# Two rounded passes for the log-decay product, in a fused gated-delta and FP4 feed-forward layer

## The reference, cut to what matters

```python
beta = sigmoid(x @ b_w.T + b_bias + beta_bias) * 2.0
g = -exp(A_log) * softplus(x @ a_w.T + dt_bias)
def step(S, inp):
    q_t, k_t, v_t, g_t, b_t = inp
    S = S * exp(g_t)[..., None, None]
    mem = einsum('bhk,bhkv->bhv', k_t, S)
    delta = (v_t - mem) * b_t[..., None]
    S = S + einsum('bhk,bhv->bhkv', k_t, delta)
    o_t = einsum('bhk,bhkv->bhv', q_t, S)
    return (S, o_t)
```

## Time and profile before

| | us |
|---|---|
| median of 3 runs | 3399.68 (3399.31 to 3400.36) |
| profiled execution, its own time | 3392.96 |
| its span, first to last instruction | 3391.1 |
| PE busy | 3166.5 (93% of the span) |
| VectorE (DVE) busy | 2422.4 (71%) |
| GpSimd (POOL) busy | 1847.1 (54%) |
| ScalarE (ACT) busy | 1671.9 (49%) |

### The profile page before, as it was taken

The page is one execution under the profiler, slowest core; times in us unless marked ns, Lnnn a source line. Parts: engine busy times, 40 slices in busy tenths (PEclk is TensorE's granted clock), DMA queues, the critical chain, the costliest instruction groups (busy, mean ns, idle before and its releaser), DMA issues.

```text
span 3391.1 us, 118358 instructions
## 1 busy us (share of the span) xinstructions
PE 3166.5 (93%) x45632; PEld 2248.8 (66%) x45632; DVE 2422.4 (71%) x5407; ACT 1671.9 (49%) x3306; POOL 1847.1 (54%) x2737
## 2 busy tenths in 40 slices
PE   5899999999999999999999999999999999999995
PEld 4666666766666766666666666666667666666664
DVE  7677776777777777767777767777777777777772
ACT  3544554545554445545445545455545455544452
POOL 3465445665455664456654456654556654466543
PEclk8999999999999999999999999999999999999996
DMA  3111111111111111111111111111111111111111
GB/s 109 39 45 27 35 42 34 45 39 27 39 37 40 45 33 30 42 33 45 45 27 36 42 33 45 40 29 36 42 36 45 35 27 42 36 42 45 27 30 29
DMA packets 318317, 132.07 MB, mean 39 GB/s; under 512 B 277089, under 2 KB 278881, under 8 KB 317793
## 3 DMA queue, kind: packets, MB, share of 16 engines
q1 hardware_dynamic: 313824, 119.26, 14.0%
q10 hardware_dynamic: 4096, 6.42, 0.5%
HBM read 75.30 MB, written 50.33 MB: 37 GB/s over the span
## 4 chain that ended last, share of the span: by engine, by line
POOL 32%; PE 32%; DMA 13%; issue 9%; DVE 6%; SPq 6%; POOLq 2%; ACT 1%; ACTq 0%; DVEq 0%
POOL arena L497 16%; POOL work L493 15%; PE PS L1210 7%; PE PS L1100 7%; DMA scr_a<-arena 5%; DMA arena<-scr_a 3%; PE PS L1196 3%; SPq L411 3%; SPq L393 3%; PE PS L1275 3%; DMA scr_t<-arena 2%; DMA arena<-scr_t 2%; PE PS L1228 2%; DVE arena L372 2%; PE PS L1246 2%
## 5 line engine op out<-in xcount | busy, mean ns | idle before, releaser
L874 DVE SCALAR_TENSOR_TENSOR arena<-PS,sc,arena 128x256 f32<-128x256 f32 x2112 | 1005.0, 482 | 301.9 <-ACT arena L594 201.1
L1132 PE MATMUL PS<-xh,wgu 128*128 128x256 f32 x2816 | 871.6, 341 | 36.1 <-DVE arena L874 35.6
L594 ACT ACTIVATE arena<-PS,sc 128x256 f32<-128x256 f32 x704 | 330.8, 475 | 760.0 <-PE PS L1133 703.0
L1133 PE MATMUL PS<-xl,wgu 128*128 128x256 f32 x2816 | 698.7, 281 | 0.0
L1145 PE MATMUL PS<-wdn,inner 128*128 128x512 f32 x1408 | 650.7, 592 | 0.0
L1132 PEld LDWEIGHTS PS<-xh,wgu 128*128 128x128 f32 x2816 | 531.4, 189 | 156.0 <-issue 87.4
L493 POOL TENSOR_TENSOR work<-arena 128x31 f32<-128x31 f32 (+15 forms) x992 | 517.5, 522 | 137.5 <-DMA arena<-scr_a 62.3
L1133 PEld LDWEIGHTS PS<-xl,wgu 128*128 128x128 f32 x2816 | 530.3, 188 | 83.2 <-issue 83.2
L497 POOL TENSOR_TENSOR arena<-arena,work 128x31 f32<-128x31 f32 (+15 forms) x992 | 543.1, 548 | 77.7
L1100 PE MATMUL PS<-xnT,wqkv 128*128 128x256 f32 x2048 | 494.9, 390 | 15.6 <-ACT inner L574 14.9
L1100 PEld LDWEIGHTS PS<-xnT,wqkv 128*128 128x128 f32 x2048 | 382.1, 193 | 83.8 <-ACT inner L574 15.9
(11 more groups left out here) (141 smaller groups left out, 4551.6 us busy)
## 6 DMA issues: line engine op xcount, KB each, us to landing
xt<-in_x SPq DMA_DIRECT2D x64, 256.0 KB, 2.8
scr_a<-arena SPq DMA_DIRECT2D x64, 256.0 KB, 2.4
arena<-scr_a SPq DMA_DIRECT2D x256, 64.0 KB, 3.3
obuf<-in_x SPq DMA_DIRECT2D x64, 256.0 KB, 2.8
scr_t<-arena SPq DMA_DIRECT2D x32, 512.0 KB, 2.7
arena<-scr_t SPq DMA_DIRECT2D x256, 64.0 KB, 2.3
out<-obuf SPq DMA_DIRECT2D x64, 256.0 KB, 2.0
wqkv<-in_wqkv ACTq DMA_DIRECT2D x1, 2048.0 KB, 12.9
```

The lines of the kernel that those rows point to most:

```text
L594: eng.activation(fa[:, u % 4, :], PS[:, bank(u, 0), 0:NB * P], ACT.Copy, scale=sc[:, u % 2, KB * m:KB * m + 1]).then_inc(fa_scaled.sem, 1)
L874: eng.scalar_tensor_tensor(out=fa[:, u % 4, :], in0=PS[:, bank(u, k // 2), k % 2 * NB * P:][:, 0:NB * P], scalar=sc[:, u % 2, KB * m + k:K ...
L1132: eng.matmul(o, w, xh[:, k, :], start=True, stop=False)
L1133: ins = eng.matmul(o, w, xl[:, k, :], start=False, stop=True)
```

## The change: what it does, and the diff

g is split into gh, g rounded to float32r, and gl = g - gh, which is exact and is float32r as well. Both are multiplied with the triangular mask (gm and gml), and `log_decay` becomes two float32r passes with a float32r copy of `later`, in place of one float32 product. gml lives in the buffer of xl. So xl can be made only when `log_decay` of both b has read gml, and its instruction moves from `split_x` to a new function `rest_of_x`, behind `keys_for_R` on POOL. E gets a place of its own in the arena, and gm's write then waits for `decay_out` of the tile before in place of `p_done`.

```diff
@@ -155,11 +156,12 @@
-        gm = sb("gm", [P, NB, H, CH])
-        E = gm
+        gm = sb("gm", [P, NB, H, CH], F32R)
...
+        gml = xl[:, :, :].rearrange("p k t -> p (k t)").rearrange("p (b h i) -> p b h i", b=NB, h=H)
+        E = arena[:, 9216:10240].rearrange("p (b h i) -> p b h i", b=NB, h=H)
@@ -433,15 +438,26 @@
             eng.tensor_copy(xh[:, :, :], xnT[:, :, :]).then_inc(xh_done.sem, 1)
+
+        def rest_of_x(eng, n):
+
             hold(eng, *xh_done.at(n, 1))
+            hold(eng, *decay_out.at(n, NB))
             eng.tensor_tensor(xl[:, :, :], xnT[:, :, :], xh[:, :, :].bitcast(F32), ALU.subtract).then_inc(xl_done.sem, 1)
 
         def masked_g(eng, t, n):
-            if t:
-                hold(eng, *p_done.at(t, NB))
-            for b in range(NB):
-                eng.tensor_tensor(gm[:, b, :, :], g[:, b, :].unsqueeze(2).broadcast_to([P, H, CH]),
-                                  tri[:, :].unsqueeze(1).broadcast_to([P, H, CH]), ALU.mult).then_inc(gm_done.sem, 1)
+
+            hold(eng, *g_done.at(n, 1))
+            eng.tensor_copy(gh[:, :, :], g[:, :, :]).then_inc(g_split.sem, 1)
+            hold(eng, *g_split.at(n, 1))
+            eng.tensor_tensor(gl[:, :, :], g[:, :, :], gh[:, :, :].bitcast(F32), ALU.subtract).then_inc(g_split.sem, 1)
+            hold(eng, *g_split.at(n, 2))
+            for part, dst in ((gh, gm), (gl, gml)):
+                if part is gh and t:
+                    hold(eng, *decay_out.at(t, NB))
+                for b in range(NB):
+                    eng.tensor_tensor(dst[:, b, :, :], part[:, b, :].bitcast(F32).unsqueeze(2).broadcast_to([P, H, CH]),
+                                      tri[:, :].unsqueeze(1).broadcast_to([P, H, CH]), ALU.mult).then_inc(gm_done.sem, 1)
@@ -530,6 +546,7 @@
                 expanded_g(eng, t, n)
                 masked_g(eng, t, n)
                 keys_for_R(eng, t, n)
+                rest_of_x(eng, n)
                 if more:
                     layer_norm_scale(eng, n.next())
@@ -1062,8 +1079,9 @@
             eng.tensor_copy(identb[:, :], ident[:, :]).then_inc(consts_done.sem, 1)
+            eng.tensor_copy(laterR[:, :], later[:, :]).then_inc(consts_done.sem, 1)
@@ -1160,10 +1178,11 @@
-                eng.wait_ge(*gm_done.at(n, b + 1))
+                eng.wait_ge(*gm_done.at(n, NB + b + 1))
                 eng.wait_ge(*cin_done.at(n, NQKV - 1 + b))
-                eng.matmul(PS[:, 4 + b, :], later[:, :], gm[:, b, :, :].rearrange("p h i -> p (h i)"), start=True,
-                           stop=False)
+                for part in (gm, gml):
+                    eng.matmul(PS[:, 4 + b, :], laterR[:, :], part[:, b, :, :].rearrange("p h i -> p (h i)"),
+                               start=(part is gm), stop=False)
                 eng.matmul(PS[:, 4 + b, :], identb[:, :], negm[:, :].unsqueeze(1).broadcast_to([P, H, CH]),
                            start=False, stop=True).then_inc(decay_out.sem, 1)
```

More of the change, by code:

```diff
@@ L117, in build @@
         negm = sb("negm", [P, CH], BF16)
+        laterR = sb("laterR", [P, P], F32R)
         identb = sb("identb", [P, P], BF16)
@@ L178, in build @@
         g = sb("g", [P, NB, H])
+        gh = sb("gh", [P, NB, H], F32R)
+        gl = sb("gl", [P, NB, H], F32R)
         bet = sb("bet", [P, NB, H])
@@ L205, in build @@
         t_read = signal("t_read", 128)
-        gm_done = signal("gm_done", 2)
+        g_split = signal("g_split", 2)
+        gm_done = signal("gm_done", 4)
         gx_done = signal("gx_done", 2)
@@ L1064, in _ @@
             eng.tensor_copy(identb[:, :], ident[:, :]).then_inc(consts_done.sem, 1)
+            eng.tensor_copy(laterR[:, :], later[:, :]).then_inc(consts_done.sem, 1)
             eng.tensor_tensor(biasS[:, :], bias[:, 0, :], bias[:, 1, :], ALU.add).then_inc(consts_done.sem, 1)
-            eng.wait_ge(consts_done.sem, 2)
+            eng.wait_ge(consts_done.sem, 3)
             eng.tensor_scalar(negm[:, :], tri[:, :], 1.0, 30000.0, ALU.subtract, ALU.mult).then_inc(consts_done.sem, 1)
@@ L1117, in half_unit @@
                             eng.wait_ge(wdn_done.sem, FM)
-                            eng.wait_ge(consts_done.sem, 6)
+                            eng.wait_ge(consts_done.sem, 7)
                 elif u == 1:
@@ L1467, in _ @@
             eng.wait_ge(zeroed.sem, 4)
-            eng.wait_ge(consts_done.sem, 4)
+            eng.wait_ge(consts_done.sem, 5)
             transpose_x(eng, Tile(0, 0, first=True), None)
```

## The result

The changed kernel takes 3417.45 us (median of 5 runs, 3416.7 to 3425.19) against 3399.68 for the kernel before, measured beside it: a ratio of 1.0055, 95% interval 1.0041 to 1.0070. The profiled execution took 3416.86 us, against 3392.96. It is slower by 18 us in the medians and 24 in the profiles.

The account below looks back on a forecast made before the run. The prediction took a chain through PE, DVE's state(0) and products(0), and the solve's ring as the bound. PE's saving and the masks counted nothing; xl's hold cost 0.66 us a step, 20.5 us, giving 3420, range 3398 to 3438.

Parts of the forecast that it names:

- the wait at `turn_kqn(0)`: PE's wait for DVE's product at turn_kqn(0), claimed to grow from 0.3 to 1.3 us a step.
- What bounds the kernel: Chain through PE, about five microseconds of DVE, back to PE at turn_kqn(0); delays from there to the Gram product lengthen steps.
- The passes on PE: Two float32r passes in log_decay on PE save 0.5 us a call, 1.0 us a step, 32 us of PE time.
- The cost of nothing: PE's log_decay saving was counted as nothing in the sum, since DVE's chain covers it.
- The split and the masks: Splitting g and two more masks on POOL: 3.2 us later, less 1 us from the front; nothing for the chain.
- xl's collision with `state(1)`: xl on POOL holds DVE's first update of S until 0.1 us behind xl's end: 1.65 us late.
- What comes late next: Second half of y_times_s(2) on PE waits for state(1): mean loss 0.66 us a step, times 31 steps, 20.5 us.
- The term for the stall: PE's "issue" stall in y_times_s(2), 0.76 us a step, hides under the new wait as far as it goes.
- The first: Rival: the update of S in state(1) isn't held by xl; 3400, within 3395 to 3405; chance 0.17.
- The second: Rival: PE's log_decay saving passes through, 32 us less or a part of it, 3368; chance 0.10.
- The third: Rival: low masks on POOL hold conv(2), 1.0 us a step at turn_qk(0), 32 us, 3432; chance 0.05.

Follow-up runs that it names:

- e1: The split alone against the kernel before: low part of g in its own buffer, xl made at the front as before; ratio 1.0010.
- e4: The kernel before with keys_for_R on POOL also waiting for products(1), float32 log decay kept; ratio 0.9996.
- e5: e1's kernel with keys_for_R on POOL also waiting for products(1); ratio 0.9997.
- e8: The changed kernel with the subtraction that makes xl replaced by two one-input copies of xnT on POOL; ratio 1.0000.
- e9: Split, xl made behind the masks, keys_for_R held until products(1), plus 96 already met waits on PE ahead of the loop; ratio 1.0029.
- e10: Split, xl made behind the masks, keys_for_R held until products(1), plus 176 already met waits on PE ahead of the loop; ratio 1.0034.
- e12: Split, xl behind the masks, keys_for_R held until products(1), gate's second part moved ahead of y_times_s(2) on PE; 3355.9 us against 3376.15, ratio 0.9942.
- e7: The changed kernel with xl made twice in a row at its place behind keys_for_R; ratio 1.0435.

## Why the prediction was right, point by point

The forecast was 3420, the range 3398 to 3438, the result 3417.45. The mechanism held too: each link from xl to the step was seen, and moving xl alone brought the loss. The saving of the passes and the wait at `turn_kqn(0)` were off, without harm, because no term of the sum hung on them.

- **What bounds the kernel.** Right. `turn_kqn(0)` starts at the same place whatever PE saves (e1), and the loss behind it is passed on in full.
- **The passes on PE.** The cost of nothing was right, the saving too large. I took 0.97 us down to 0.5. The two passes take 1717.52 - 1716.95 = 0.57 from start to start, so 0.4 a call is saved. My reason was incomplete: I named DVE's products as the cover and took PE's slack for 0.3 us. That was a misreading of rows 4: of its 10.1 us, 8.9 are waits of PE's weight loads (PEld), which run ahead of the matmuls. The matmuls themselves stood still for 0.07 us in front of `turn_kqn(0)`. With that cover removed (e4, e5) the recurrence and the lack of instructions still stood there. The expected wait of 1.3 us did not appear: it grew from 0.07 to 0.22 us, and the rest of the 0.8 us saved went into `y_times_s(1)` and `k_times_u(1)`. That the saving was worth nothing was right by the cover that I named and by one that I didn't see.
- **The split and the masks.** Right. POOL was done with the masks 1706.44 - 1699.82 = 6.6 us behind `t_times_r`'s start, I had 7.0, and the convolution behind g took 3.73 us in place of 4.33. The halo copy's median fell from 2204 to 182 ns, as the reading of its end against xl's end had said. `turn_qk(0)` starts 6.29 us behind `t_times_r`, as before.
- **xl's collision with `state(1)`.** Right in place and kind, and the terms were near: 1.65 us late was forecast, 1.77 measured. xl took 2.53 us here, not 2.35, and the update ended 0.08 behind it where I had 0.1. The halo copy L976 was weak support for it, since it is a copy with one input; L372 and `conv` have two in SBUF, like the update. My limit to two-input products on POOL was wrong: copies hold it as well (e8).
- **What comes late next.** I forecast a mean loss of 0.66 us a step, measured 0.76 (0.77 at `y_times_s(2)`). Times 31 that is 23.6, which is the 23.9 between the two profiles; between the medians it is 17.8. The term for the stall that hides part of the wait (0.76) was needed, without it the sum would have been 44 us.
- **The rivals.** The first (update not held) fell with the longest update of 2056 ns. The second (PE's saving passes through) fell with e1. The third (masks hold the convolution) fell with e1 and the 3.73 us.

## What to carry to other kernels

Before work is moved on POOL, look up what DVE does at its new place. Here each product and copy on POOL from SBUF to SBUF held a DVE update with two SBUF inputs until it ended, however short that one is, and if that one sits in a recurrence, everything waits. DVE operations with an input in PSUM ran on beside it, and a power on POOL held nothing. What counts is how much of the POOL instruction is left when the DVE operation comes: with two copies of 1.2 and 1.0 us in place of one subtraction of 2.5, `state(1)` was 0.81 us late in place of 1.77. A saving on the busiest engine counts only where the chain runs through it, and covers come in layers: here DVE's products, the recurrence and PE's lack of instructions lay within a few tenths of a microsecond of each other, and only treating the last gave the time. Where PE waits for "issue" in a burst of short products, putting slow ones in front of the burst gave 0.7 us a step here.

## What the runs showed of the hardware that was not expected

- A wait of PE for "issue" moves with instructions put ahead of the loop (e9, e10), and goes when slow products stand in front of the burst (e12): 0.7 us a step.
- One-input copies on POOL hold a DVE update with two SBUF inputs to their end too, as a subtraction does: the update ends 0.07 to 0.08 us behind either (e8, changed kernel). A power on POOL of 5.44 us held no such operation (L520 beside L886).
- PE's stalls for "issue" end 1.2 to 1.7 us behind the landing of a 16 KB packet of the instruction queue (before, e9).
- A PE that was busy for 2.31 of 5 us had a mean clock of 0.66 in the next 5 us, which nearly doubled the price of a wait, 4.7 us a step for one of 2.45 (e7).
- A float32r pass of 512 columns takes 0.34 and 0.23 us from start to start in the log decay, a float32 product of the same size 0.97.
